# A delta-rule recurrence in chunks: TensorE's, ScalarE's and GpSimd's work put in another order around three crossings

## The chip, the cores and the metric

One core of a Trainium2 chip runs the whole kernel. The metric is the device time of one execution in microseconds (us); the time of a kernel is the median of its runs.

## The reference, cut to what matters

Four layers follow each other on `x` (4 x 1024 x 128, f32). The change touches only the first, a gated delta rule with 16 heads of 64 by 64 state:

```python
q = silu(causal_dwconv(x @ Wq.T)); k = silu(causal_dwconv(x @ Wk.T)) * SCALE
v = silu(causal_dwconv(x @ Wv.T)); a = sigmoid(x @ Wa.T + ba); beta = sigmoid(x @ Wb.T + bb)
def step(S, inp):
    qt, kt, vt, at, bt = inp
    err = einsum('bhij,bhj->bhi', S, kt) - vt
    S = at[..., None] * S - bt[..., None, None] * (err[..., None] * kt[:, :, None, :])
    return S, einsum('bhij,bhj->bhi', S, qt)
o = (layernorm(o, over 64) * ln_w + ln_b) * sigmoid(x @ Wg.T);  return o @ Wo.T
```

The other three (a mixture of experts, banded attention, local attention with its feed-forward) run after it and are left alone.

## The kernel before, in words

Class `DeltaRule` cuts the 1024 steps into 32 chunks of 32 steps (`SEG`), all 4 batches and 16 heads at once, and each chunk into 4 quarters of 8 steps. The five engines run lists written out by hand (`tensor`, `vector`, `scalar`, `gpsimd`, `sync`), in order, and wait for each other only on semaphores. In the names below s is the chunk; `old`, `older` and `nxt` are s-1, s-2 and s+1.

What VectorE does in one chunk is a chain. `dve_P` (L1261) turns the product P of the state with k and q out of banks 4 and 5. Four quarters of single steps follow (`dve_quarter`, L1299 to L1305). After each of the first three comes a **crossing**, which carries a finished quarter over to the steps behind it: VectorE turns W (L1324, into `a_wt`), TensorE multiplies it with the Gram matrix (`pe_cross`, L676, 64 products in banks 6 and 7), and VectorE turns the result (L1347, into `a_cross`). Between L1324 and L1347 VectorE has one to three other operations. After the last quarter `dve_state` turns W once more (L1378), TensorE forms the update U (`pe_U`, L705), ScalarE writes two quarters of the new state (L866), VectorE adds the other two (L1385), and TensorE can form P of the next chunk (`pe_P`, L660: a first half for batches 0 and 1 that waits for ScalarE's part, a second that waits for VectorE's).

Beside this chain TensorE prepares the next chunk and finishes older ones, in the gaps between crossings: projections of a, k, q and v (L572, L559), time rows (L594), Gram products (L584), turns of the normed output (`pe_turn`, L604), the output gate (`pe_gate`, L559 with `a_w_g`), the output product (`pe_out`, L634) and two sums for the norm (L619). These results go to banks 0 and 1 in turn: `take` hands out bank n % 2 and waits until ScalarE has emptied the result two before it. `act_gram` empties one Gram bank with six activations (L799, L801, four on L805); there are two banks per chunk. GpSimd (`pool_...`) makes decays, the rest of P and the output's products. The chain ends for chunk s when the new P is there, so a chunk's length is the distance of two L1261 of channel half 0.

`pe_P` also waits for `("dev", s - 2)`, the second sum of the norm, which VectorE takes at the very end of `dve_state`:

```python
self.dve_out(e, q, s, 1)          # L1371, waits for GpSimd's s_pq (s, 1)
for n in range(2, 4): ...         # L1385, the state
self.dve_values(e, q, s + 1)      # L1228
self.dve_moment(e, q, s - 1, "dev")   # L1244
```

Of the kernel before, what the change touches and what calls it, by code (L numbers as in the profile page):

```python
# [442 lines left out]
class DeltaRule:  # L443
# [194 lines left out]
    def pe_P(self, e, q, s, ch):  # L638
# [7 lines left out]
        else:  # L646
# [4 lines left out]
            if s >= 3:  # L651
                q.wait_ge(self.s_evac, ("out", s - 3))
# [57 lines left out]
    def tensor(self, e, q):  # L710
# [5 lines left out]
        for half in range(2):  # L716
            self.pe_gram(e, q, 0, half)
            self.pe_project_rows(e, q, "v", 0, half)
        for s in range(self.nseg):
            old, older, nxt = s - 1, s - 2, s + 1  # L720
# [35 lines left out]
            self.pe_U(e, q, s)  # L756
        for s in (self.nseg - 2, self.nseg - 1):
# [30 lines left out]
    def act_gram(self, e, q, s, par):  # L788

        heads = slice(8 * par, 8 * par + 8)  # L790
        v = self.held(("gram", s, par)).rearrange("p (r c t z) -> p c r z t", z=2, c=NCK, t=CK)
        dst = self.G1[:, :, :, heads].rearrange("p z t r -> p r z t")
        q.wait_ge(self.s_full, ("gram", s, par))
        if s:
# [3 lines left out]
        rows_of = self.cst["cross_rows"]  # L798
        e.activation(self.Gh[:, :, :, heads].rearrange("p z t r -> p r z t"), v[:, 1], ACT.Identity, scale=rows_of[:, 2:3],  # L799
                     bias=rows_of[:, 3:4]).then_inc(*self.s_gh.at((s, par)))  # L800
# [2263 lines left out]
```

## Time and profile before

| | us |
|---|---|
| median of 3 runs (4098.43 to 4113.96) | 4102.49 |
| the profiled execution | 4110.15 |
| its span in the trace | 4108.4 |
| TensorE, VectorE, GpSimd, ScalarE busy | 3193.8, 2963.0, 2255.2, 2106.6 |
| the recurrence's chunks, start of the first to start of the last | 151 to 2472 |

The span is the profile's own clock from first to last instruction; the execution's time is 1.75 us more. The busy times are over all four layers. The recurrence is read on the timeline of single chunks, which are alike from the fourth on.

### The profile page before, as it was taken

How to read it: one execution, taken by the hardware profiler on the slowest of the kernel's cores; microseconds unless marked ns; L12 is line 12 of the kernel's file. 1: busy time of each engine (PE TensorE's matmuls, PEld its weight loads, DVE VectorE, ACT ScalarE, POOL GpSimd, SP SyncE). 2: the span in 40 equal slices, each digit the busy share in tenths (PEclk: the TensorE clock that was granted, in tenths of full speed). 3: DMA queues.
4: the chain of work that ended last, by engine and by line, in shares of the span. 5: the costliest groups of instructions: out<-in, count | busy, mean ns of one | idle time of the engine just before them, and what ended most of it. 6: DMA issues, size and time to landing. Idle time of an engine off the chain costs nothing. (4 is left out here: it accounts for less than half of the span.)

```text
span 4108.4 us, 125735 instructions
## 1 busy us (share of the span) xinstructions
PE 3193.8 (78%) x53313; PEld 2381.3 (58%) x53313; DVE 2963.0 (72%) x6568; ACT 2106.6 (51%) x4454; POOL 2255.2 (55%) x2831
## 2 busy tenths in 40 slices
PE   4777777677777777777777774468999979998998
PEld 2566565565565655655655654355666647655775
DVE  4587777777787777777877875216888868856885
ACT  2334434444444444443444442335888879937982
POOL 1466666676666666666766765332000068807860
PEclk7888888888888888888888886588999989998999
DMA  2000100100100100001000000510000011101110
GB/s 72 18 29 17 29 19 17 31 17 16 31 17 17 31 17 23 25 17 29 15 15 27 15 15 15 149 41 1 2 2 2 2 34 38 43 6 38 40 37 26
DMA packets 131379, 105.91 MB, mean 26 GB/s; under 512 B 56784, under 2 KB 100044, under 8 KB 130562
## 3 DMA queue, kind: packets, MB, share of 16 engines
q1 hardware_dynamic: 128514, 95.15, 8.7%
q8 instruction: 421, 6.90, 0.7%
q0 software_dynamic: 2304, 2.71, 0.2%
q14 instruction: 140, 1.15, 0.1%
HBM read 62.57 MB, written 16.30 MB: 19 GB/s over the span
## 5 line engine op out<-in xcount | busy, mean ns | idle before, releaser
L1299 DVE TENSOR_TENSOR a_tmp<-a_h,banks 128x128 f32<-128x128 f32 (+6 forms) x896 | 439.2, 490 | 32.9
L1305 DVE TENSOR_REDUCE a_h<-a_tmp 128x64 f32<-128x128 f32 (+6 forms) x896 | 434.4, 485 | 8.8
L1347 DVE STREAM_TRANSPOSE a_cross<-banks 128x1024 f32<-128x1024 f32 x96 | 120.0, 1250 | 309.7 <-PE banks L676 309.7
L660 PE MATMUL banks<-a_st,a_kq 64*32 64x64 f32 x8192 | 179.2, 280 | 176.3 <-DVE a_variance L1244 131.6
L775 ACT ACTIVATE a_kq<-banks 128x512 f32<-128x512 f32 x128 | 82.9, 648 | 392.7 <-PE banks L559 392.7
L978 POOL TENSOR_TENSOR a_h<-a_h,a_a 128x128 f32<-128x128 f32 (+3 forms) x256 | 140.9, 550 | 250.1 <-DVE a_h L1305 250.1
L2196 ACT ACTIVATE c_s<-c_s,c_low 128x384 f32<-128x384 f32 (+1 forms) x512 | 266.3, 579 | 18.9 <-DVE c_low L2140 13.6
L660 PEld LDWEIGHTS banks<-a_st,a_kq 64*32 64x32 f32 x8192 | 166.2, 145 | 188.2 <-DVE a_variance L1244 135.8
L784 ACT ACTIVATE a_va<-banks 128x512 f32<-128x512 f32 x128 | 134.1, 1086 | 274.9 <-PE banks L572 274.8
L559 PEld LDWEIGHTS banks<-a_xseg,a_w_k 128*128 128x128 f32 x2048 | 236.5, 194 | 60.0 <-ACT a_va L784 41.5
L2140 DVE CUSTOM_DVE_ANT_0 c_s<-banks,c_band 128x384 f32<-128x384 f32 (+1 forms) x512 | 245.4, 517 | 24.8 <-PE banks L2065 24.8
L559 PE MATMUL banks<-a_xseg,a_w_k 128*128 128x128 f32 x2048 | 242.6, 278 | 26.2 <-DMA a_xseg<-xn 18.3
L2241 POOL TENSOR_TENSOR c_qm<-c_qT,c_heads 128x512 f32<-128x512 f32 x32 | 33.3, 1040 | 398.4 <-PE banks L2065 398.1
L572 PE MATMUL banks<-a_w_v,a_xseg 128*32 128x512 f32 x2048 | 245.5, 622 | 6.6 <-ACT a_g L805 5.3
L1066 POOL TENSOR_TENSOR a_cross<-a_cross,a_dk 128x128 f32<-128x128 f32 x96 | 54.3, 566 | 338.8 <-DVE a_cross L1347 338.8
L2079 PE MATMUL banks<-k_ident,c_s 128*128 128x128 f32 x1408 | 217.8, 285 | 28.4 <-ACT c_pt L2203 15.6
L559 PE MATMUL banks<-a_xseg,a_w_q 128*128 128x128 f32 x2048 | 234.0, 273 | 0.0
L559 PEld LDWEIGHTS banks<-a_xseg,a_w_q 128*128 128x128 f32 x2048 | 231.3, 191 | 0.2 <-ACT a_kt L824 0.2
L2079 PEld LDWEIGHTS banks<-k_ident,c_s 128*128 128x128 f32 x1408 | 155.4, 143 | 120.0 <-ACT c_s L2196 111.1
L2577 ACT ACTIVATE d_S<-d_S,d_low 128x128 f32<-128x128 f32 x512 | 199.2, 399 | 19.3 <-DVE d_low L2642 18.9
L2426 PE MATMUL banks<-d_wqkv,d_hT 128*128 128x512 f32 x384 | 199.8, 635 | 10.2 <-DVE d_rot L2624 5.9
L1303 DVE TENSOR_TENSOR a_h<-a_h,banks 128x32 f32<-128x32 f32 (+6 forms) x640 | 178.6, 279 | 22.0
(327 smaller groups left out, 9223.8 us busy)
## 6 DMA issues: line engine op xcount, KB each, us to landing
a_ab<-decays SPq DMA_DIRECT2D x256, 128.0 KB, 3.0
d_Vs<-d_V SPq DMA_DIRECT2D x128, 128.0 KB, 2.4
sent<-k_nothing SPq DMA_DIRECT2D x40, 64.5 KB, 2.1
b_xe<-sent SPq DMA_DIRECT2D x8, 322.5 KB, 3.4
a_xseg<-xn SPq DMA_DIRECT2D x32, 70.0 KB, 2.9
a_xrow<-in_L_attn_x SPq DMA_DIRECT2D x128, 16.0 KB, 1.9
x<-a_xrow SPq DMA_DIRECT2D x128, 16.0 KB
back<-k_nothing SPq DMA_DIRECT2D x32, 64.0 KB, 1.6
```

The lines of the kernel that those rows point to most:

```text
L559: t = e.matmul(b[:, m * SW:(m + 1) * SW].rearrange("p (b t) -> p b t", b=NB), self.wT[n][:, j, ct * P:(ct + 1) * P], xs[:, :, off:off + SE ...
L572: t = e.matmul(b[bi * SEG:(bi + 1) * SEG, :], xs[:, bi, off:off + SEG], self.wT[n][:, j, part], start=(j == 0), stop=(j == taps - 1))
L660: t = e.matmul(pb[bi * SEG:(bi + 1) * SEG, at:at + DK], kq[ps, ct * NB + bi, js].rearrange("p t z -> p (t z)"), self.ST[ps, bi * NCT + ct, ...
L978: e.tensor_tensor(self.history(t + 1, lo, t), self.history(t, lo, t), at, ALU.mult).then_inc(*self.s_hist.at((s, t)))
L1299: e.tensor_tensor(prod, both, gram, ALU.mult).then_inc(*step.at((s, t, "product")))
L1303: e.tensor_tensor(self.history(t, lo, t), self.history(t, lo, t), at, ALU.mult).then_inc(*step.at((s, t, "decay")))
L1305: e.tensor_reduce(self.results(t), prod, AX.X, ALU.add).then_inc(*step.at((s, t, "w")))
L2079: t = e.transpose(b[:, j * P:(j + 1) * P], self.S[u % self.NS][:, j * P:(j + 1) * P], self.c.ident[:])
L2140: e.tensor_tensor_reduce(out=self.S[u % self.NS][:, 0:w], in0=self.c.bank(r)[:, 0:w], in1=self.W.band[:, m0:m0 + w], scale=-HD ** -0.5, sc ...
L2196: e.activation(s[:, 0:w], s[:, 0:w], ACT.Exp, scale=-1.0, bias=self.low[u % self.NS][:, 0:1]).then_inc(*self.s_exp.at(u))
L2426: e.matmul(b, self.hT[:, g * P:(g + 1) * P], self.W.wqkv[:, z * INNER:(z + 1) * INNER], start=True, stop=True).then_inc(*self.s_proj.at((g ...
L2577: t = e.activation(s, s, ACT.Exp, scale=-1.0, bias=self.low[g % 2][:, par, r:r + 1], accum_out=self.rows[g % 2][:, par, r:r + 1])
```

## The change

TensorE gets its work around the crossings in another order: time rows ahead of k, half of k behind crossing 0, both gates and no v ahead of crossing 2, and the output product of chunk s-3 (not s-2) between Gram and turns. ScalarE follows that order and empties both Gram banks with six activations of twice the width; the first user of a bank after Gram waits for both. GpSimd makes the output's products one chunk later, around `pool_rest`, and some of its other steps change places. VectorE's list differs at one place, the end of `dve_state`. SyncE's row transfers move a chunk.

```diff
-            q.wait_ge(self.s_evac, self.ring[n - 2])
+            last = self.ring[n - 2]
+            q.wait_ge(self.s_evac, ("gram", last[1], 1) if last[0] == "gram" else last)
...
 def tensor
             self.pe_P(e, q, s, 0)
             self.pe_P(e, q, s, 1)
             if more:
                 for half in range(2):
                     self.pe_project_rows(e, q, "a", nxt, half)
-                for half in range(2):
-                    self.pe_project(e, q, "k", nxt, half)
-            self.pe_cross(e, q, s, 0)
             for n in range(2):
                 self.pe_time_rows(e, q, s, n)
+            if more:
+                self.pe_project(e, q, "k", nxt, 0)
+            self.pe_cross(e, q, s, 0)
             if old >= 0:
                 self.pe_moment(e, q, old, "mean")
             if more:
+                self.pe_project(e, q, "k", nxt, 1)
                 for half in range(2):
                     self.pe_project(e, q, "q", nxt, half)
             self.pe_cross(e, q, s, 1)
             if more:
                 for n in range(2):
                     self.pe_gram(e, q, nxt, n)
+            if oldest >= 0:
+                self.pe_out(e, q, oldest)
             if older >= 0:
                 for n in range(2):
                     self.pe_turn(e, q, older, n)
                 for n in range(2):
                     self.pe_gate(e, q, older, n)
-            if more:
-                self.pe_project_rows(e, q, "v", nxt, 0)
             self.pe_cross(e, q, s, 2)
             if more:
-                self.pe_project_rows(e, q, "v", nxt, 1)
-            if older >= 0:
-                self.pe_out(e, q, older)
+                for half in range(2):
+                    self.pe_project_rows(e, q, "v", nxt, half)
...
 def act_gram (one call for both banks)
+        e.activation(to(self.Gh), v[:, 1], ACT.Identity, scale=rows_of[:, 2:3], bias=rows_of[:, 3:4]).then_inc(*self.s_gh.at(s))
+        e.activation(to(self.G1), v[:, 1], ACT.Copy, scale=-1 / 8).then_inc(*self.s_gwhole.at(s))
+        q.wait_ge(self.s_gwhole, s)
         for bi in range(NB):
             rows = slice(bi * SEG, bi * SEG + CK)
-            t = e.activation(dst[rows], v[rows, 0], ACT.Copy, scale=-1 / 8)
-        t.then_inc(*self.s_evac.at(("gram", s, par)))
+            t = e.activation(to(self.G1)[rows], v[rows, 0], ACT.Copy, scale=-1 / 8)
+            if bi >= 2:
+                t.then_inc(*self.s_evac.at(("gram", s, bi - 2)))
...
 def gpsimd
+            if oldest >= 0:
+                self.pool_gate(e, q, oldest, 0)
             self.pool_rest(e, q, s)
+            if oldest >= 0:
+                self.pool_gate(e, q, oldest, 1)
...
             self.pool_cross(e, q, s, 3)
-            if old >= 0:
-                self.pool_centre(e, q, old, 1)
-            for half in range(2):
-                if older >= 0:
-                    self.pool_gate(e, q, older, half)
             self.pool_older(e, q, s, 1)
...
+                self.pool_gram_rows(e, q, nxt)
+                self.pool_prepare(e, q, nxt, 0)
+            if oldest >= 0:
+                self.pool_add(e, q, oldest)
             self.pool_query(e, q, s, 1)
...
 def dve_state
         self.dve_last(e, q, s, 1)
-        self.dve_out(e, q, s, 1)
+        if s:
+            self.dve_moment(e, q, s - 1, "dev")
+        if s + 1 < self.nseg:
+            self.dve_values(e, q, s + 1)
         for n in range(2, 4):
...
-        if s + 1 < self.nseg:
-            self.dve_values(e, q, s + 1)
-        if s:
-            self.dve_moment(e, q, s - 1, "dev")
+        self.dve_out(e, q, s, 1)
```

TensorE around crossings 0 and 1 of one chunk, before (`a_gx` marks crossings 0 and 2, `a_gh` crossing 1):

```order
L572 MATMUL banks<-a_w_a,a_xseg 32x512 x8
L559 MATMUL banks<-a_xseg,a_w_k 128x128 x32
L676 MATMUL banks<-a_wt,a_gx 32x64 x64
L594 MATMUL banks<-k_ident,a_kq 32x128 x32
L619 MATMUL banks<-a_o_1,k_row_mean 128x128 x8
L559 MATMUL banks<-a_xseg,a_w_q 128x128 x32
L676 MATMUL banks<-a_wt,a_gh 32x64 x64
```

and of the change:

```order
L574 MATMUL banks<-a_w_a,a_xseg 32x512 x8
L596 MATMUL banks<-k_ident,a_kq 32x128 x32
L561 MATMUL banks<-a_xseg,a_w_k 128x128 x16
L678 MATMUL banks<-a_wt,a_gx 32x64 x64
L621 MATMUL banks<-a_o_1,k_row_mean 128x128 x8
L561 MATMUL banks<-a_xseg,a_w_k 128x128 x16
L561 MATMUL banks<-a_xseg,a_w_q 128x128 x32
L678 MATMUL banks<-a_wt,a_gh 32x64 x64
```

Half of k moved behind crossing 0, the time rows ahead of it.

TensorE from Gram to the second sum of the norm, around crossing 2, before:

```order
L584 MATMUL banks<-a_kq 32x64 x64
L604 MATMUL banks<-k_ident,a_o 128x128 x8
L559 MATMUL banks<-a_xseg,a_w_g 128x128 x8
L572 MATMUL banks<-a_w_v,a_xseg 32x512 x16
L676 MATMUL banks<-a_wt,a_gx 32x64 x64
L572 MATMUL banks<-a_w_v,a_xseg 32x512 x16
L634 MATMUL banks<-a_w_o,a_y 128x128 x8
L619 MATMUL banks<-a_o,k_row_mean 128x128 x8
```

and of the change:

```order
L586 MATMUL banks<-a_kq 32x64 x64
L636 MATMUL banks<-a_w_o,a_y 128x128 x8
L606 MATMUL banks<-k_ident,a_o 128x128 x8
L561 MATMUL banks<-a_xseg,a_w_g 128x128 x8
L678 MATMUL banks<-a_wt,a_gx 32x64 x64
L574 MATMUL banks<-a_w_v,a_xseg 32x512 x32
L621 MATMUL banks<-a_o,k_row_mean 128x128 x8
```

One half of v moved from ahead of the crossing to behind it, the output product from behind it to the place behind Gram.

VectorE at the end of a chunk, before:

```order
L1378 STREAM_TRANSPOSE a_wt<-a_h 128x32x32
L1361 TENSOR_TENSOR a_tmp<-a_h,banks 128x256
L1363 TENSOR_REDUCE a_h<-a_tmp 128x32
L1371 TENSOR_TENSOR a_o_1<-a_p_1,a_h 128x32x16
L1385 TENSOR_TENSOR a_st<-a_st,banks 128x512 x2
L1228 STREAM_TRANSPOSE a_bv<-a_va 128x1024
L1244 TENSOR_REDUCE a_variance<-banks 128x32
```

and of the change:

```order
L1391 STREAM_TRANSPOSE a_wt<-a_h 128x32x32
L1374 TENSOR_TENSOR a_tmp<-a_h,banks 128x256
L1376 TENSOR_REDUCE a_h<-a_tmp 128x32
L1257 TENSOR_REDUCE a_variance<-banks 128x32
L1241 STREAM_TRANSPOSE a_bv<-a_va 128x1024
L1401 TENSOR_TENSOR a_st<-a_st,banks 128x512 x2
L1384 TENSOR_TENSOR a_o_1<-a_p_1,a_h 128x32x16
```

The output's subtraction (L1371, now L1384) moved from the first place behind the quarter to the last, the sum and the turn of v ahead of the state's additions.

## Rows read from the trace of the kernel before

**Rows 1.** Timeline of VectorE, first L1261 of the fourth and of the last chunk

```profile
360.51 1.25 DVE L1261 STREAM_TRANSPOSE a_p<-banks 128x1024 f32<-128x1024 f32 x1 [3.36 <-PE banks L660]
...
2472.24 1.25 DVE L1261 STREAM_TRANSPOSE a_p<-banks 128x1024 f32<-128x1024 f32 x1 [3.13 <-PE banks L660]
```

**Rows 2.** Groups of VectorE, 287 to 2472 us: busy us, mean ns | idle before, releaser

```profile
L1347 DVE STREAM_TRANSPOSE a_cross<-banks 128x1024 f32<-128x1024 f32 x87 | 108.7, 1250 | 292.5 <-PE banks L676 292.5
...
L1261 DVE STREAM_TRANSPOSE a_p<-banks 128x1024 f32<-128x1024 f32 x58 | 71.3, 1229 | 95.5 <-PE banks L660 95.5
...
L1371 DVE TENSOR_TENSOR a_o<-a_p,a_h 128x512 f32<-128x512 f32 x58 | 66.5, 1147 | 52.3 <-POOL a_p L1084 52.3
```

**Rows 3.** Timeline of VectorE, one chunk: start, us, instruction [idle before, releaser]

```profile
1039.43 1.25 DVE L1261 STREAM_TRANSPOSE a_p<-banks 128x1024 f32<-128x1024 f32 x1 [3.36 <-PE banks L660]
...
1056.17 1.25 DVE L1347 STREAM_TRANSPOSE a_cross<-banks 128x1024 f32<-128x1024 f32 x1 [2.78 <-PE banks L676]
...
1071.30 1.25 DVE L1347 STREAM_TRANSPOSE a_cross<-banks 128x1024 f32<-128x1024 f32 x1 [0.19 <-PE banks L676]
...
1091.18 1.25 DVE L1347 STREAM_TRANSPOSE a_cross<-banks 128x1024 f32<-128x1024 f32 x1 [6.09 <-PE banks L676]
...
1102.05 1.94 DVE L1378 STREAM_TRANSPOSE a_wt<-a_h 128x1024 f32<-128x1024 f32 x1
...
1106.49 1.44 DVE L1371 TENSOR_TENSOR a_o<-a_p,a_h 128x512 f32<-128x512 f32 x1 [1.80 <-POOL a_p L1084]
1107.86 1.27 DVE L1385 TENSOR_TENSOR a_st<-a_st,banks 128x512 f32<-128x512 f32 x2
...
1113.66 1.25 DVE L1261 STREAM_TRANSPOSE a_p<-banks 128x1024 f32<-128x1024 f32 x1 [3.21 <-PE banks L660]
```

**Rows 4.** Timeline of TensorE, the same chunk

```profile
1046.69 7.41 PE L559 MATMUL banks<-a_xseg,a_w_k 128*128 128x128 f32 x64 [0.34 <-ACT a_va L784]
1054.03 2.06 PE L676 MATMUL banks<-a_wt,a_gx 32*32 32x64 f32 x128
...
1059.80 7.31 PE L559 MATMUL banks<-a_xseg,a_w_q 128*128 128x128 f32 x64
1069.17 2.07 PE L676 MATMUL banks<-a_wt,a_gh 32*32 32x64 f32 x128 [2.06 <-issue]
...
1073.71 0.77 PE L584 MATMUL banks<-a_kq 64*32 64x64 f32 x40 [1.21 <-issue]
...
1079.79 1.12 PE L604 MATMUL banks<-k_ident,a_o 128*128 128x128 f32 x4 [2.62 <-ACT a_g L805]
1081.33 3.78 PE L559 MATMUL banks<-a_xseg,a_w_g 128*128 128x128 f32 x16 [0.42 <-ACT a_oT L882]
1085.04 4.08 PE L572 MATMUL banks<-a_w_v,a_xseg 128*32 128x512 f32 x32
...
1104.04 2.00 PE L705 MATMUL banks<-a_wt,a_kt 32*64 32x64 f32 x128 [1.10 <-DVE a_wt L1378]
1110.51 3.08 PE L660 MATMUL banks<-a_st,a_kq 64*32 64x64 f32 x128 [4.48 <-DVE a_variance L1244]
```

**Rows 5.** Timeline of ScalarE, the same chunk

```profile
1045.57 1.98 ACT L784 ACTIVATE a_va<-banks 128x512 f32<-128x512 f32 x2 [6.76 <-PE banks L572]
...
1072.34 0.80 ACT L799 ACTIVATE a_gh<-banks,k_cross_rows 128x256 f32<-128x256 f32 x1 [1.45 <-PE banks L584]
...
1077.31 2.43 ACT L805 ACTIVATE a_g<-banks 16x256 f32<-16x256 f32 x4
1079.77 2.91 ACT L882 ACTIVATE a_oT<-banks,a_lnb,a_lnw 128x128 f32<-128x128 f32 x8
...
1105.26 1.08 ACT L866 ACTIVATE a_st<-banks 128x512 f32<-128x512 f32 x2 [5.52 <-PE banks L705]
```

**Rows 6.** Timeline of TensorE, P in another chunk

```profile
739.56 1.89 PE L660 MATMUL banks<-a_st,a_kq 64*32 64x64 f32 x128 [1.38 <-DVE a_p L1261]
```

**Rows 7.** Stretches of 3 us: busy us of each engine, granted TensorE clock, DMA

```profile
1078.00:1081.00 3.00, 1.12 (x4) 0.72 (x4) 2.86 (x5) 2.95 (x7) 1.68 (x3) 0.50 0.00 0
...
1087.00:1090.00 3.00, 3.00 (x84) 1.31 (x80) 0.00 (x0) 0.85 (x2) 0.00 (x0) 1.00 0.02 5
```

More of the change, by code:

```diff
@@ L745, in tensor @@
                     self.pe_gate(e, q, older, n)
-            if more:
-                self.pe_project_rows(e, q, "v", nxt, 0)
             self.pe_cross(e, q, s, 2)
             if more:
-                self.pe_project_rows(e, q, "v", nxt, 1)
-            if older >= 0:
-                self.pe_out(e, q, older)
+                for half in range(2):
+                    self.pe_project_rows(e, q, "v", nxt, half)
             if old >= 0:
@@ L756, in tensor @@
             self.pe_U(e, q, s)
+        if self.nseg >= 3:
+            self.pe_out(e, q, self.nseg - 3)
         for s in (self.nseg - 2, self.nseg - 1):
@@ L786, in act_project_rows, with act_gram @@
                      ACT.Sigmoid if n == "a" else ACT.Silu).then_inc(*self.s_evac.at((n, s, half)))
[L788 to L793, printed above, removed]
+    def act_gram(self, e, q, s):
+        assert self.slot[("gram", s, 0)] % 2 == 0
+        v = self.c.bank(0, 2).rearrange("p (r c t z) -> p c r z t", z=2, c=NCK, t=CK)
+        to = lambda x: x[:].rearrange("p z t r -> p r z t")
+        rows_of = self.cst["cross_rows"]
+        for par in range(2):
+            q.wait_ge(self.s_full, ("gram", s, par))
         if s:
@@ L919, in scalar @@
             if more:
+                self.act_project(e, q, "k", nxt, 0)
+            self.act_cross_gram(e, q, s, 2)
+            if more:
+                self.act_project(e, q, "k", nxt, 1)
                 for half in range(2):
@@ L924, in scalar @@
             if more:
-                for n in range(2):
-                    self.act_gram(e, q, nxt, n)
+                self.act_gram(e, q, nxt)
+            if oldest >= 0:
+                self.act_out(e, q, oldest)
             if older >= 0:
@@ L936, in scalar @@
             if more:
-                self.act_cross_gram(e, q, nxt, 0)
-                self.act_project_rows(e, q, "v", nxt, 1)
-            if older >= 0:
-                self.act_out(e, q, older)
+                for half in range(2):
+                    self.act_project_rows(e, q, "v", nxt, half)
             self.act_state(e, q, s)
@@ L1176, in gpsimd @@
             self.pool_cross(e, q, s, 2)
+            self.pool_from_half(e, q, s)
             for t in range(2 * QK + HAND, 3 * QK):
                 self.pool_history(e, q, s, t)
-            self.pool_from_half(e, q, s)
             self.pool_next(e, q, s, 1)
-            if old >= 0:
-                self.pool_centre(e, q, old, 0)
+            for half in range(2):
+                if old >= 0:
+                    self.pool_centre(e, q, old, half)
             self.pool_cross(e, q, s, 3)
-            if old >= 0:
-                self.pool_centre(e, q, old, 1)
-            for half in range(2):
-                if older >= 0:
-                    self.pool_gate(e, q, older, half)
             self.pool_older(e, q, s, 1)
@@ L1192, in gpsimd @@
                 self.pool_cumulate(e, q, nxt, 2, QK)
+                self.pool_gram_rows(e, q, nxt)
+                self.pool_prepare(e, q, nxt, 0)
+            if oldest >= 0:
+                self.pool_add(e, q, oldest)
             self.pool_query(e, q, s, 1)
             if more:
-                self.pool_prepare(e, q, nxt, 0)
-                self.pool_gram_rows(e, q, nxt)
                 self.pool_values(e, q, nxt)
-            if older >= 0:
-                self.pool_add(e, q, older)
+        if self.nseg >= 3:
+            for half in range(2):
+                self.pool_gate(e, q, self.nseg - 3, half)
+            self.pool_add(e, q, self.nseg - 3)
         if self.nseg >= 2:
@@ L1455, in sync @@
         self.spread_decays(e, q, 0)
-        for s in range(self.nseg + 2):
+        for s in range(self.nseg + 3):
             if s + 1 < self.nseg:
@@ L1460, in sync @@
                 self.load(e, s + 1)
-            if s >= 2:
-                self.get_rows(e, q, s - 2)
-            self.fill.piece(e, s)
+            if s >= 3:
+                self.get_rows(e, q, s - 3)
+            if s < self.nseg + 2:
+                self.fill.piece(e, s)
             if s + 1 < self.nseg:
```

37 lines of the change are left out of this document (16 added, 21 removed).

## The prediction

> **What bounds the kernel now.** I read the timeline of VectorE first, from the fourth chunk's P to the last one's [rows 1]: 2472.24 - 360.51 = 2111.7 us for 28 chunks, 75.4 us each. That is half of the span, and it is the only part that the change touches. Then the groups of VectorE with the idle time before them [rows 2]: over 29 chunks it waits 292.5 us for the crossings, 95.5 for P and 52.3 for GpSimd's query part, together 440, or 15.2 us a chunk. The rest, some 60 us, is VectorE's own work, so VectorE is the bound with gaps in it, and no order of the other engines gives back more than those 15.2.
>
> One chunk shows where the gaps lie [rows 3]. I call T the start of L1261, X0, X1 and X2 the three starts of L1347, and w the end of L1378 (1102.05 + 1.94 = 1103.99). The legs are T to X0 16.7 (waits 2.78), X0 to X1 15.1 (0.19), X1 to X2 19.9 (6.09), X2 to w 12.8, w to the next T 9.7 (1.80 and 3.21); sum 74.2. The timeline of TensorE says why [rows 4]. Crossing 0 starts at 1054.03, right behind the k projection, though its operand was ready before: TensorE was late. Crossing 1 starts after 2.06 us of idle time, as soon as its operand is there. Behind it come Gram, turns that wait for ScalarE, gates and half of v, and crossing 2 can start only when that half (1085.04 + 4.08) is done. At the chunk's end, P of the next one waits 4.48 us until VectorE has done the norm's sum.
>
> **The change, leg by leg.** Instruction counts stay, but for ScalarE's Gram copies, six fewer a chunk.
>
> *T to X0.* Half of k (7.41 / 2 = 3.7) leaves the place ahead of crossing 0, and the time rows come there, 1.9 (they and the mean's sum fill the 3.8 us between crossing 0 and q, two like pieces) [rows 4]. Crossing 0, at T + 14.6, could start at T + 12.8, X0 at T + 14.95. P ahead of it takes 3.1 us in most chunks and 1.89 in one where the clock was full [rows 4, 6]; with that, TensorE is early, and VectorE's own end of work sets X0: 1056.17 - 2.78 is T + 13.95. The a projection's wait for its transfer goes as well, since GpSimd's add, behind which SyncE issues that transfer, now stands ahead of its query part and not behind its values. I take 14.3, between 13.95 and 14.95.
>
> *X0 to X1.* TensorE has between crossings 0 and 1 now the mean 1.9, half of k 3.7 and q 7.3, 12.9 us; VectorE's turned W comes 12.9 us after X0 (crossing 1 starts at 1069.17, X0 at 1056.17). The 2 us of slack are used up. 15.1 stays; from 15.1 to 16.5.
>
> *X1 to X2.* The new list up to crossing 2: Gram ends 3.2 us after X1 (1073.71 + 0.77), a stall of 1.21 in it [rows 4]. ScalarE took from 1072.34 to 1079.74 for twelve copies of 256 columns [rows 5], 0.6 each. The six of 512 are not in the trace. The nearest row is L784, 512 columns with a strided output: 1.98 for two [rows 5]. I take 0.98 each and 6.0 for six; the ends are 3.9 (0.65 each, as if the stride cost nothing) and 7.3 (twice 0.6 each). The output product of s-3, 2.05, hides beside them. So the banks are free at X1 + 9.3, and both turns wait for that. A turn is 1.12 at the low clock, four of the eight copies on L882 1.5, a gate half of 3.78: 9.4 + 1.1 + 1.5 + 1.9 + 1.9 = X1 + 15.8 [rows 4, 5], crossing 2 is 2.06, X2 = X1 + 18.0; without the stall 16.9. VectorE is free at X1 + 13.8 (1091.18 - 6.09), so it still waits some 4 us. I take 17.6 instead of 19.9. What pays is not the shorter emptying alone: 4.1 us of v are no longer ahead of the crossing.
>
> The Trainium skill's page "ScalarE: Activation LUTs" (section "What ACT_TABLE_LOAD costs") gives an activation with immediate operands as 186 ns plus 0.833 ns a column. For 256 columns that is 0.40 us where the trace shows 0.6, so the row speaks against it for these strided copies. By the page the six would take 3.7 us and X2 would come 2.3 us earlier, about 65 us over the kernel.
>
> *X2 to w* stays at 12.8. Behind crossing 2 TensorE has v 7.3, the norm's sum 2 and the carry 1.9, 11.2 in all, and 1.6 of slack before U. GpSimd's chain to the query's end keeps its length: two halves of y and one centring leave it, the Gram rows, the preparation and the add come into it, about 3.8 against 3.7 us.
>
> *w to T.* VectorE's last reduction ends at w + 0.7 (1106.49 - 1.80). Now the norm's sum (0.24) and v's turn (1.2) follow, during U's 2.00 us, then the state's additions, 1.27, to w + 3.4 [rows 3, 4]. ScalarE's half of the state is there at w + 2.35 [rows 5], so the first half of P runs beside the additions and the second ends at w + 4.4 at full clock, w + 5.6 at low. The subtraction that waited for GpSimd is last: 1.44, to w + 4.8; GpSimd's query part, which it met at w + 2.5 before, is long done by then. I take 4.9 instead of 9.7; from 4.8 to 5.7.
>
> New chunk: 14.3 + 15.15 + 17.6 + 12.8 + 4.9 = 64.75. The average chunk before was 1.2 above the one I read, from transfer waits and stalls of TensorE; I keep half, 65.4. That is 10.0 less for 28 chunks, 281. The first three chunks gain mostly at their ends, the last one at crossing 0, 20 together; behind the loop the output of one more chunk is left, +3. Sum: 4110.2 - 298 = 3812 for the profiled execution. It lay 7.7 above the median, so 3804.
>
> **The rivals.**
> - *Full clock between the crossings.* If TensorE keeps 2.4 GHz through turns and gates, these halve: turn 0.56, a gate 0.95, and P at the full clock. X1 to X2 becomes 15.6, T to X0 14.0, the chunk 63.0: 12.4 x 28 + 20 = 367 less, 3736. Against it: the granted clock was 0.50 there after idle times of 2 to 3 us [rows 7], and the change leaves one of some 4 us in the same place. Chance 0.12.
> - *TensorE is the bound.* With no slack ahead of crossings 0 and 1, every stall like the 1.21 in Gram [rows 4] is on the path, and turns and gates are. Three more a chunk, 1.1 each, make 68.7: 6.7 x 28 + 15 = 203 less, 3900. For it: the average chunk before is 1.2 us above the one read [rows 1, 3], so such stalls are there. Chance 0.25.
> - *The low clock stays (slower).* The idle time between the output product and the turns lets the clock fall to 1.2 GHz, as rows 7 show at 1078; before, it was back at 1.00 at 1087. If it came back only behind U, v, sum and carry would take 22 us, U would be 9.4 us late and P 0.8: the gain is gone. If it also stayed low through part of k and q of the next chunk, each microsecond of that work costs one more, and 1 to 2 us a chunk give about +40, 4145. It decides from the point at which the low stretch, some 10 us before, lasts over 20. Against it: P now follows U almost at once, where the clock used to fall too. Chance 0.05.
> - *No change.* The waits return elsewhere, GpSimd the likeliest place, since its list is as long as before in a shorter chunk. Chance 0.03.
>
> The Trainium skill's page "TensorE: Matmul & The Clock Gate" (section "The HAM clock gate") calls the throttled state the default, released by activity; that is the ground of the slower rival, and the trace agrees that the clock falls behind idle stretches.
>
> **How the numbers follow.** The forecast has 0.55, with 3770 to 3850 as its own range. Predicted time 3804. The range 3735 to 3900 takes in the full clock on one side and the stalls on the other. Below 0.5% (20 us) a measurement of this kernel tells nothing; faster is the first three cases, 0.92, same 0.03, slower 0.05.
>
> **What would show it.** In the profile after: distance of P to P about 65 us; idle before L1347 about 0.5, 0.5 and 4 us; no wait of P for the norm's sum; VectorE's output subtraction without idle time; the strided Gram copies near 1 us each; turns behind both Gram banks. Wrong, if crossing 1 waits for q by more than 1 us on average, if the copies take 0.65, if the clock row between Gram and gates reads 1.00, or if w to T stays above 7.

## The result, and the profile after

| | before | changed |
|---|---|---|
| median, us | 4102.53 (4 runs) | 3905.78 (4 runs, 3899.87 to 3914.52) |
| profiled execution, us | 4110.15 | 3908.86 |
| TensorE, VectorE, GpSimd, ScalarE busy, us | 3193.8, 2963.0, 2255.2, 2106.6 | 3193.8, 2970.4, 2258.5, 2078.5 |

The ratio is 0.9518, its 95% interval 0.9491 to 0.9545: 4.8% faster. The forecast was 3804 and the range ended at 3900, 6 us short. Busy times hardly moved, so all of it is waiting. The timeline of VectorE in the changed kernel, with the first L1274 (the old L1261) of the fourth and the last chunk, and between them the main rows of one chunk; L1360 is the old L1347, L1391 the old L1378, L1401 the old L1385, L1384 the old L1371:

```profile
355.41 1.25 DVE L1274 STREAM_TRANSPOSE a_p<-banks 128x1024 f32<-128x1024 f32 x1 [1.99 <-PE banks L662]
...
966.00 1.25 DVE L1274 STREAM_TRANSPOSE a_p<-banks 128x1024 f32<-128x1024 f32 x1 [1.61 <-PE banks L662]
...
981.01 1.25 DVE L1360 STREAM_TRANSPOSE a_cross<-banks 128x1024 f32<-128x1024 f32 x1 [1.07 <-PE banks L678]
996.20 1.25 DVE L1360 STREAM_TRANSPOSE a_cross<-banks 128x1024 f32<-128x1024 f32 x1 [0.19 <-PE banks L678]
...
1014.54 1.25 DVE L1360 STREAM_TRANSPOSE a_cross<-banks 128x1024 f32<-128x1024 f32 x1 [4.67 <-PE banks L678]
1025.42 1.99 DVE L1391 STREAM_TRANSPOSE a_wt<-a_h 128x1024 f32<-128x1024 f32 x1
...
1029.50 1.29 DVE L1401 TENSOR_TENSOR a_st<-a_st,banks 128x512 f32<-128x512 f32 x2
1030.70 1.77 DVE L1384 TENSOR_TENSOR a_o<-a_p,a_h 128x512 f32<-128x512 f32 x1
...
1034.12 1.25 DVE L1274 STREAM_TRANSPOSE a_p<-banks 128x1024 f32<-128x1024 f32 x1 [1.65 <-PE banks L662]
...
2262.28 1.25 DVE L1274 STREAM_TRANSPOSE a_p<-banks 128x1024 f32<-128x1024 f32 x1 [2.15 <-PE banks L662]
```

(2262.28 - 355.41) / 28 = 68.1 us a chunk, against 75.4 [rows 1]. The same reading of all 28 chunks, fourth to last but one, gives the legs that the prediction used (T the start of P's turn, X0 to X2 the starts of the three crossings' turns, w the end of the last turn of W, taken in every run as its start + 1.94 us as in [rows 3]; in the changed kernels that turn lasts up to 0.1 us longer, so that the true X2 to w is that much longer and w to T that much shorter):

| mean of a leg, us | before | forecast | after |
|---|---|---|---|
| T to X0 | 17.07 | 14.3 | 14.76 |
| X0 to X1 | 15.41 | 15.15 | 15.23 |
| X1 to X2 | 20.38 | 17.6 | 18.46 |
| X2 to w | 12.81 | 12.8 | 12.83 |
| w to T | 9.75 | 4.9 | 6.83 |
| chunk | 75.42 | 64.75, with stalls 65.4 | 68.10 |

The groups of VectorE, 287 to 2262 us, answer to [rows 2]: waits for crossings 292.5 to 168.0, for P 95.5 to 43.5, for GpSimd's query part 52.3 to nothing.

```profile
L1360 DVE STREAM_TRANSPOSE a_cross<-banks 128x1024 f32<-128x1024 f32 x87 | 108.7, 1250 | 168.0 <-PE banks L678 167.3
L1384 DVE TENSOR_TENSOR a_o<-a_p,a_h 128x512 f32<-128x512 f32 x59 | 72.4, 1226 | 0.0
L1274 DVE STREAM_TRANSPOSE a_p<-banks 128x1024 f32<-128x1024 f32 x58 | 71.2, 1228 | 43.5 <-PE banks L662 43.5
```

The sum: 28 chunks give 28 x 7.32 = 205 us, the first three 10. Ahead of the loop 5.1 are lost (the first P is turned at 156.55 instead of 151.45: v now waits for both Gram banks), behind the last chunk's w 5.2, and 3.5 in the other layers. 205 + 10 - 14 = 201, the difference of the two profiled executions. Ahead of the loop TensorE stands idle for 6.4 us ahead of v, until ScalarE has emptied Gram.

TensorE in the chunk above, to be laid beside [rows 4]:

```profile
975.11 3.84 PE L561 MATMUL banks<-a_xseg,a_w_k 128*128 128x128 f32 x32
978.87 2.07 PE L678 MATMUL banks<-a_wt,a_gx 32*32 32x64 f32 x128
...
994.08 2.06 PE L678 MATMUL banks<-a_wt,a_gh 32*32 32x64 f32 x128 [0.44 <-issue]
...
998.90 0.64 PE L586 MATMUL banks<-a_kq 64*32 64x64 f32 x29 [1.34 <-issue]
...
1006.01 1.97 PE L606 MATMUL banks<-k_ident,a_o 128*128 128x128 f32 x8 [4.48 <-ACT a_g L811]
1008.72 3.75 PE L561 MATMUL banks<-a_xseg,a_w_g 128*128 128x128 f32 x16 [0.74 <-ACT a_oT L889]
1012.40 2.07 PE L678 MATMUL banks<-a_wt,a_gx 32*32 32x64 f32 x128
...
1027.47 2.00 PE L707 MATMUL banks<-a_wt,a_kt 32*64 32x64 f32 x128 [2.29 <-DVE a_wt L1391]
1029.92 2.59 PE L662 MATMUL banks<-a_st,a_kq 64*32 64x64 f32 x100 [0.46 <-ACT a_st L873]
1033.01 1.07 PE L662 MATMUL banks<-a_st,a_kq 64*32 64x64 f32 x28 [0.50 <-issue]
```

Crossing 0 still starts right behind k, but behind half of it. Crossing 1 has 0.4 us of idle time ahead of it where it had 2. Crossing 2 starts right behind the gates, which are slow. P follows U after 0.46, is slow too, and stops once inside. The stretches say how fast the clock was (columns as in [rows 7]):

```profile
1002.00:1005.00 3.00, 0.00 (x0) 0.00 (x0) 2.83 (x6) 2.95 (x4) 1.32 (x3) 1.00 0.00 0
1005.00:1008.00 3.00, 1.97 (x8) 1.57 (x8) 2.93 (x3) 2.07 (x5) 2.84 (x4) 0.58 0.01 3
1008.00:1011.00 3.00, 2.28 (x10) 2.28 (x11) 1.87 (x3) 2.98 (x7) 3.00 (x3) 0.50 0.00 0
1026.00:1029.00 3.00, 1.53 (x112) 1.53 (x114) 2.97 (x5) 0.30 (x1) 2.84 (x6) 1.00 0.50 169
1029.00:1032.00 3.00, 2.54 (x126) 2.43 (x121) 2.97 (x4) 2.48 (x7) 2.76 (x3) 0.56 0.60 186
```

It fell to 1.2 GHz (0.50) in the 4.5 us idle ahead of the turns. It fell again near the end of U, which has 2.3 us of idle time ahead of it, in the middle of the chain's end. ScalarE in the same chunk:

```profile
999.64 1.24 ACT L806 ACTIVATE a_gh<-banks,k_cross_rows 128x512 f32<-128x512 f32 x1 [3.84 <-PE banks L586]
...
1001.80 4.16 ACT L811 ACTIVATE a_g<-banks 16x512 f32<-16x512 f32 x4
```

Six wide copies, 999.64 to 1005.96: 6.3 us, about 1.05 each, near the 6.0 forecast.

### The profile page after: what moved, and what is told of

It is laid out like the page before. It is cut to its first block and busy times, and to the rows that moved or that the text cites. A ratio compares the mean times of both kernels' runs of the same rounds, so it can differ in the third digit from the quotient of the medians.

```text
span 3907.1 us, 125601 instructions
## 1 busy us (share of the span) xinstructions
PE 3193.8 (82%) x53313; PEld 2407.0 (62%) x53313; DVE 2970.4 (76%) x6568; ACT 2078.5 (53%) x4262; POOL 2258.5 (58%) x2831
## 5 line engine op out<-in xcount | busy, mean ns | idle before, releaser
L789 ACT ACTIVATE a_va<-banks 128x512 f32<-128x512 f32 x128 | 135.3, 1108 | 243.8 <-PE banks L574 243.8
L1360 DVE STREAM_TRANSPOSE a_cross<-banks 128x1024 f32<-128x1024 f32 x96 | 120.0, 1250 | 185.1 <-PE banks L678 184.3
L561 PE MATMUL banks<-a_xseg,a_w_k 128*128 128x128 f32 x2048 | 244.8, 276 | 17.6 <-DMA a_xseg<-xn 17.6
L662 PE MATMUL banks<-a_st,a_kq 64*32 64x64 f32 x8192 | 195.1, 284 | 75.8 <-DVE a_p L1274 44.1
L574 PE MATMUL banks<-a_w_v,a_xseg 128*32 128x512 f32 x2048 | 229.4, 600 | 6.4 <-ACT a_g L811 6.4
L662 PEld LDWEIGHTS banks<-a_st,a_kq 64*32 64x32 f32 x8192 | 175.9, 148 | 93.6 <-DVE a_p L1274 50.8
L1337 DVE STREAM_TRANSPOSE a_wt<-a_h 128x1024 f32<-128x1024 f32 x96 | 191.3, 1993 | 3.3
```

The lines of the kernel that those rows point to most:

```text
L561: t = e.matmul(b[:, m * SW:(m + 1) * SW].rearrange("p (b t) -> p b t", b=NB), self.wT[n][:, j, ct * P:(ct + 1) * P], xs[:, :, off:off + SE ...
L574: t = e.matmul(b[bi * SEG:(bi + 1) * SEG, :], xs[:, bi, off:off + SEG], self.wT[n][:, j, part], start=(j == 0), stop=(j == taps - 1))
L662: t = e.matmul(pb[bi * SEG:(bi + 1) * SEG, at:at + DK], kq[ps, ct * NB + bi, js].rearrange("p t z -> p (t z)"), self.ST[ps, bi * NCT + ct, ...
L1337: e.transpose(self.Wt[:].rearrange("p x i -> p i x"), self.W).then_inc(*self.s_wm.at((s, n)))
```

## The experiments

All ratios are to the kernel before, run beside the variant on the same chip; the change itself is 0.9518 (0.9491 to 0.9545). Legs are means over the same 28 chunks.

### Undoing one part at a time

**state_old**: the old order at the end of `dve_state`.

```diff
         self.dve_last(e, q, s, 1)
-        if s:
-            self.dve_moment(e, q, s - 1, "dev")
-        if s + 1 < self.nseg:
-            self.dve_values(e, q, s + 1)
+        self.dve_out(e, q, s, 1)
...
-        self.dve_out(e, q, s, 1)
+        if s + 1 < self.nseg:
+            self.dve_values(e, q, s + 1)
+        if s:
+            self.dve_moment(e, q, s - 1, "dev")
```

> The change, but with the old order at the end of dve_state (output subtraction first, norm's sum last). If the new order is what shortens w to the next P (9.75 us before, 6.83 after), that leg comes back to 9 to 9.7 us and the time to about 3905 + 29 x 2.5 = 3980. Rival: the leg is short because GpSimd's query part is done earlier and VectorE no longer waits for it; then the old order costs little, since the subtraction does not wait: leg about 8, time about 3935.

0.9621 (0.9599 to 0.9643), median 3951.57. w to T went to 8.89 us, T to X0 fell a little, to 14.31. The leg lies just below the first forecast, the time between the two. So the order is worth 2.06 us of that leg, but 1.5 of the chunk (69.62): part of it is eaten up at crossing 0. The leg's other 0.86 us of gain do not hang on the order; with the old order the subtraction still waits for GpSimd, 36.8 us in all instead of 52.3.

**v_ahead**: the first half of v ahead of crossing 2, on TensorE and ScalarE.

```diff
+            if more:
+                self.pe_project_rows(e, q, "v", nxt, 0)
             self.pe_cross(e, q, s, 2)
             if more:
-                for half in range(2):
-                    self.pe_project_rows(e, q, "v", nxt, half)
+                self.pe_project_rows(e, q, "v", nxt, 1)
... (ScalarE's list likewise)
```

> The change with the first half of v back ahead of crossing 2 on TensorE and ScalarE. If v ahead of the crossing is what cost the old X1 to X2, the crossing comes 3.7 to 4.1 us later: X1 to X2 about 22.3, time about 3905 + 29 x 3.8 = 4015, nearly the whole gain of that leg and more. Rival: TensorE would have that time again behind the crossing; it has slack there, so nothing comes back. Within 1% of 3905 only if the gates and not v set crossing 2.

0.9778 (0.9752 to 0.9804), median 4016.39; X1 to X2 22.37, 3.9 us more, and T to X0 14.32, 0.4 less; the chunk is 3.56 longer. As expected: what stands ahead of the crossing in the list is paid nearly in full.

**k_ahead**: both halves of k ahead of crossing 0.

```diff
                 self.pe_project(e, q, "k", nxt, 0)
+                self.pe_project(e, q, "k", nxt, 1)
             self.pe_cross(e, q, s, 0)
...
-                self.pe_project(e, q, "k", nxt, 1)
... (ScalarE's list likewise)
```

> The change with both halves of k ahead of crossing 0. T to X0 grows by 3.7 us less the slack that is there, from 14.8 to about 18.0; X0 to X1 stays 15.2 (TensorE then has 3.7 us of slack ahead of crossing 1). Time about 3905 + 29 x 3.2 = 3998. Rival: the slack gained ahead of crossing 1 gives something back; time below 3960.

0.9778 (0.9752 to 0.9805), median 4014.21; T to X0 18.29, X0 to X1 16.04, X1 to X2 17.66. The first figure is as expected; the other two were not forecast, and nearly cancel. The traces say where they come from. TensorE now stands idle for 3.94 us ahead of crossing 1:

```profile
1040.70 2.81 PE L678 MATMUL banks<-a_wt,a_gh 32*32 32x64 f32 x128 [3.94 <-issue]
```

The granted clock is 0.65 on average in that crossing, where it is 1.00 in the change, and its products take 2.99 us instead of 2.07. Behind it Gram's issue waits, here in k_ahead and then in the change, are nearly gone:

```profile
L586 PE MATMUL banks<-a_kq 64*32 64x64 f32 x3712 | 76.7, 263 | 1.4 <-issue 1.4
```

```profile
L586 PE MATMUL banks<-a_kq 64*32 64x64 f32 x3712 | 63.7, 222 | 31.5 <-issue 31.5
```

The chunk is 3.46 longer. The three parts undone by themselves (order, v, k) cost 8.5 us of a chunk together, more than the 7.32 of the whole change, so they are not independent of each other.

**gram_narrow**: both banks emptied together, by twelve copies of 256 columns.

```diff
+        h = (slice(0, 8), slice(8, 16))
...
+            e.activation(to(self.G1)[rows, h[0]], v[rows, 0, h[0]], ACT.Copy, scale=-1 / 8)
+            t = e.activation(to(self.G1)[rows, h[1]], v[rows, 0, h[1]], ACT.Copy, scale=-1 / 8)
```

> The change with both Gram banks emptied together, but by twelve copies of 256 columns instead of six of 512. If the wide copies save 1.1 us a chunk (7.4 against 6.3 us in the traces) and the turns wait for their end, X1 to X2 grows from 18.5 to 19.6 and the time by 29 x 1.1 = 32 us, to about 3937. Rival: the gain of the joined emptying lies elsewhere; within 10 us of the change.

0.9511 (0.9487 to 0.9535): no difference. ScalarE's timeline shows first and last of the twelve:

```profile
1069.22 0.78 ACT L807 ACTIVATE a_gh<-banks,k_cross_rows 128x256 f32<-128x256 f32 x1 [3.69 <-PE banks L586]
...
1075.04 0.62 ACT L815 ACTIVATE a_g<-banks 16x256 f32<-16x256 f32 x1
```

1069.22 to 1075.66 is 6.44 us, against 6.32 for six wide ones. The narrow ones start 0.40 and 0.65 us after each other in turn, though each lasts 0.6. My expectation took 7.4 for twelve from the old trace; that was the time of two separate emptyings, in which the copies ran one behind the other. In this order of twelve the width brings nothing.

**pool_old**: GpSimd's old order behind crossing 2 and for Gram rows and preparation.

```diff
-            self.pool_from_half(e, q, s)
             for t in range(2 * QK + HAND, 3 * QK):
                 self.pool_history(e, q, s, t)
+            self.pool_from_half(e, q, s)
...
-                self.pool_gram_rows(e, q, nxt)
-                self.pool_prepare(e, q, nxt, 0)
             if oldest >= 0:
                 self.pool_add(e, q, oldest)
             self.pool_query(e, q, s, 1)
             if more:
+                self.pool_prepare(e, q, nxt, 0)
+                self.pool_gram_rows(e, q, nxt)
```

> The change with GpSimd's list back in the old order at two places: the rest of the half chunk behind the four histories and the second centring behind crossing 3; Gram rows and preparation behind the query part. If GpSimd was never what the chain waits for, nothing changes (within 10 us of 3905). Rival: X2 waits for the rest of the half (from_half), or ScalarE's bank of Gram rows for the next chunk comes too late and holds the first quarter; 20 us or more slower.

0.9514 (0.9498 to 0.953), median 3906.98: GpSimd's order at these places is free. Its y one chunk later, and the output product with it, was not undone by itself.

**add_late**: GpSimd's add behind the values.

```diff
-            if oldest >= 0:
-                self.pool_add(e, q, oldest)
             self.pool_query(e, q, s, 1)
             if more:
                 self.pool_values(e, q, nxt)
+            if oldest >= 0:
+                self.pool_add(e, q, oldest)
```

> The change with GpSimd's add back behind the values, at the end of its chunk. The add releases SyncE, which then issues the transfer of a_xseg. If its earlier place is needed for the change to pay, the a projection waits for the transfer again, about 3 us a chunk: T to X0 from 14.8 to about 17.5, time about 3905 + 29 x 2.7 = 3983. Rival: with the output product in the middle of the chunk SyncE is early enough in any case; within 10 us of 3905.

0.9525 (0.9509 to 0.9541), median 3912.55. The wait for a_xseg came back in 14 of 28 chunks, 14.1 us in all, and T to X0 rose by 0.4. The rival was right: in this kernel the place of the add matters little.

### One part alone: a gain that goes elsewhere

**state_alone**: the kernel before with only the new end of `dve_state` (the diff of that function as it stands in the change).

> The kernel before with only the new order at the end of dve_state. If the order itself gives the shorter end of the chunk, w to P falls from 9.75 to 6.5 to 7 us with everything else as before, time 4111 - 29 x 3 = about 4024. Rival: without GpSimd's earlier query part and the idle crossings the end is bound elsewhere; w to P above 8.5, time above 4075.

0.9986 (0.9974 to 0.9998), median 4099.95. This is the most telling run. w to T fell from 9.75 to 6.14 us, even below the 6.5 to 7 expected, and T to X0 rose from 17.07 to 20.80. TensorE's timeline in a chunk of state_alone shows the new wait:

```profile
1032.45 1.89 PE L660 MATMUL banks<-a_st,a_kq 64*32 64x64 f32 x128 [1.37 <-DVE a_p L1261]
1038.67 3.64 PE L572 MATMUL banks<-a_w_a,a_xseg 128*32 128x512 f32 x16 [4.33 <-DMA a_xseg<-xn]
```

The transfer is issued by SyncE behind the row stores of chunk s-2, and these wait for GpSimd's add, last in its list, which did not move. P came 3.6 us earlier, the a projection did not, and in the idle time the clock fell too (3.64 us instead of 1.93; granted clock 0.50 in the stretch 1039 to 1042).

**state_load**: state_alone, and the load ahead of the row stores.

```diff
+        self.load(e, 1)
         for s in range(self.nseg + 2):
-            if s + 1 < self.nseg:
-                if s >= 3:
-                    q.wait_ge(self.s_full, ("g", s - 3, 1))
-                self.load(e, s + 1)
...
+            if s + 2 < self.nseg:
+                if s >= 2:
+                    q.wait_ge(self.s_full, ("g", s - 2, 1))
+                self.load(e, s + 2)
             if s >= 2:
                 self.put_rows(e, q, s - 2)
```

> The kernel before with the new order at the end of dve_state, and with SyncE's load of a_xseg for the chunk after next issued ahead of the row stores (so that it waits no longer for GpSimd's add). In state_alone the 3.6 us saved at the chunk's end came back as a later X0, with the a projection waiting 3.2 us for that transfer. If the transfer is the cause, T to X0 falls from 20.8 to about 17, w to P stays near 6.1, time 4100 - 29 x 3.8 = about 3990. Rival: the k projection itself is late because it starts a fixed time after P; then P, a and k all simply start earlier and the time is near 4000 as well only if P runs at full clock; at the low clock T to X0 stays above 19 and the time above 4045.

0.9754 (0.9738 to 0.9771), median 4005.56; T to X0 16.66, w to T 6.16, chunk 71.29. The transfer was the cause of the lost gain: the same edit that was worth nothing is worth 2.3% once the load is moved ahead in the queue. The earlier load alone, in the kernel before, was not run; there the a projection waits for its transfer 27.4 us in all, 0.7% of the time, so it could give little more than that by itself. The a projection's groups in state_alone and state_load, 287 to 2262 us:

```profile
L572 PE MATMUL banks<-a_w_a,a_xseg 128*32 128x512 f32 x432 | 88.2, 956 | 80.8 <-DMA a_xseg<-xn 80.8
```

```profile
L572 PE MATMUL banks<-a_w_a,a_xseg 128*32 128x512 f32 x448 | 63.3, 680 | 16.9 <-DMA a_xseg<-xn 15.6 <-issue 1.2
```

### The chunk's end: clock or stalls

**small_ab**: the decays' transfers made small.

```diff
...
+                if s:
+                    src, dst = src[:, 0:32], dst[:, 0:32]
...
```

> The change, with the transfers that spread the decays over the partitions cut from 128 KB to 8 KB each from the second chunk on (their count and waits stay; the decays of the state are then wrong). Theory B, TensorE's stalls marked 'issue' inside P come from instruction delivery that shares the DMA engines with these transfers: the stalls in P go, w to P falls from 6.8 to about 6.0, time about 3880. Theory A, P is slow because the granted clock fell to 1.2 GHz in the 2.3 us of idle time before U: nothing changes by more than 0.3%.

0.9483 (0.9461 to 0.9504), median 3894.55; w to T 6.47. P's issue waits went from 18.6 to 14.9 us. That is neither of the two forecasts: the traffic has a small share at most, and the intervals overlap with the change's.

**warm_u** and **warm_t**: products of the identity that nobody uses, in TensorE's idle time ahead of U, or ahead of the turns.

```diff
+    def pe_warm(self, e, q, s, n, bank):
+        ...
+        for _ in range(n):
+            e.matmul(b[:, 384:512], self.c.ident[:], self.c.ident[:], start=True, stop=True)
...
             self.pe_carry(e, q, s)
+            self.pe_warm(e, q, s, 8, 5)
             self.pe_U(e, q, s)
```

> The change, with 8 extra products of the identity (about 1.8 us at full clock, into bank 5, used by nobody) between the carry and U, in TensorE's idle time. Theory A (the clock falls in that idle time, and P then runs at 1.2 GHz): the granted clock stays at 1.00 through U and P, P takes about 1.9 us of work instead of 3.6, w to P falls from 6.83 to 5.1 to 5.5 us and T to X0 from 14.76 to about 14.1, time about 3905 - 29 x 2.2 = 3842. Theory B (instruction delivery): w to P stays above 6.3, time within 0.5% of 3905.

0.9476 (0.9454 to 0.9497), median 3894.55. w to T only 6.43: P ran at the faster clock in most chunks, and waited longer inside. The interval touches that of the change.

> The change, with 14 extra products of the identity (about 3.2 us at full clock, into bank 4, used by nobody) before the turns, where TensorE stands idle 4.5 us while ScalarE empties Gram. If the clock is what makes turns and gates slow there: both turns 1.0 instead of 2.0 us, both gates 1.9 instead of 3.75, X1 to X2 from 18.46 to about 16.5, time about 3905 - 29 x 2 = 3847. If ScalarE's norm copies and not the clock set the gates: X1 to X2 stays above 17.8, time above 3885.

0.9432 (0.941 to 0.9453), median 3872.25. X1 to X2 17.49, between the two forecasts: both turns took 1.1 instead of 2.0 us, but the gates, with 1.2 us of idle time ahead of them, were at the low clock again in 15 of 28 chunks.

**thin_U** and **thin_warm**: U without 7 of 8 head pairs of batches 0 and 1, so that their state is not updated; the second with warm_u's products as well.

```diff
+                        if pair == 0 and ct < NCT - 1:
+                            continue
```

> The change with 56 of the 64 products of U that belong to batches 0 and 1 in pairs left out (7 of 8 head pairs; their state is then not updated). The waits marked issue come in bursts of small products: Gram's behind crossing 1, P's behind U. If they are TensorE's instruction supply running behind a burst, P's wait for issue (18.6 us in 28 chunks, longest 2.5) nearly vanishes, Gram's stays at 1.1 a chunk, and w to P falls from 6.8 to about 5.5. Rival, the decays' transfers or anything tied to the time of day in the chunk: P's issue wait stays.

One run, 3863.76: w to T 5.56, as expected.

> thin_U and warm_u together: no burst of U ahead of P, and TensorE busy ahead of U. My step that failed said that the chunk's end would take 4.9 us, with P at full clock and without stall; it takes 6.8. thin_U alone gave 5.6, warm_u alone 6.4. If clock and supply stall together are the whole cause, both away give P's 1.9 us of work without issue wait, and the leg is set by VectorE's subtraction, 5.1 us or less. If it stays at 5.5 or above, something else is in it.

One run, 3854.54: w to T 5.26, between the two forecasts (5.1 and 5.5). P's groups, 290 to 2200 us, in the change, in warm_u, in thin_U and in thin_warm:

```profile
L662 PE MATMUL banks<-a_st,a_kq 64*32 64x64 f32 x7296 | 174.0, 284 | 68.0 <-DVE a_p L1274 39.5 <-issue 18.6 <-ACT a_st L873 9.7
```

```profile
L662 PE MATMUL banks<-a_st,a_kq 64*32 64x64 f32 x7216 | 150.4, 257 | 87.6 <-DVE a_p L1285 38.6 <-issue 36.0 <-ACT a_st L884 12.9
```

```profile
L662 PE MATMUL banks<-a_st,a_kq 64*32 64x64 f32 x7284 | 167.5, 276 | 49.8 <-DVE a_p L1276 39.3 <-ACT a_st L875 4.5 <-issue 4.0
```

```profile
L662 PE MATMUL banks<-a_st,a_kq 64*32 64x64 f32 x7191 | 135.4, 235 | 76.7 <-DVE a_p L1287 45.4 <-DVE a_st L1414 13.1 <-issue 11.8
```

Work and issue waits of one P (128 records) come to 3.38 us in the change, 3.31 in warm_u, 3.01 in thin_U and 2.62 in thin_warm. A faster clock alone turns work into waiting; a shorter burst ahead of P alone leaves P slow; both together bring 0.76 us. That is still above the 1.9 us without a wait that were expected: issue waits are left (11.8 us), and a wait for VectorE's additions (13.1) is new. But P is hardly late any more. The idle time ahead of its turns is 4.4 us in all, against 42.2 in the change, and in 18 of 28 chunks there is none:

```profile
1015.08 1.25 DVE L1287 STREAM_TRANSPOSE a_p<-banks 128x1024 f32<-128x1024 f32 x1 [0.29 <-PE banks L662]
```

```profile
L1287 DVE STREAM_TRANSPOSE a_p<-banks 128x1024 f32<-128x1024 f32 x57 | 69.8, 1225 | 4.4 <-PE banks L662 4.2
```

There VectorE's own subtraction ends the leg in most chunks. A thinner U is also 0.6 us shorter, so not all of the 1.3 us between 6.83 and 5.56 is stall.

### A version that beats both

**warm_all** fills three idle stretches, **wide_warm** the same with fewer, wider products, **wide_pro** has v ahead of Gram before the loop besides.

```diff
+            self.pe_warm(e, q, s, 14, 4)   # ahead of pe_turn
+            self.pe_warm(e, q, s, 4, 4)    # ahead of pe_gate
+            self.pe_warm(e, q, s, 7, 5)    # ahead of pe_U
```

> The change with extra products of the identity in three idle stretches: 14 ahead of the turns, 4 between turns and gates, 7 ahead of U. If the clock is all that makes these places slow: gates at 1.9 instead of 3.75 us, X1 to X2 16.3, w to P 6.3, T to X0 14.5, chunk 65.1, time about 3905 - 29 x 3.0 = 3818. Rival: the extra instructions lengthen the supply stalls (as in warm_u: P's issue waits 36 instead of 19 us) and ScalarE's norm copies set the gates; chunk above 66.5, time above 3860.

0.9336 (0.9319 to 0.9353), median 3838.24; X1 to X2 16.72, w to T 6.39, chunk 65.76; the time lies between the two forecasts. At turns and gates the clock stays, and a gate's products go from 427 to 286 ns each:

```profile
1050.00:1053.00 3.00, 1.58 (x14) 1.39 (x14) 2.86 (x5) 2.50 (x5) 2.18 (x4) 1.00 0.00 0
1053.00:1056.00 3.00, 2.49 (x20) 2.11 (x19) 3.00 (x3) 2.98 (x8) 2.92 (x4) 1.00 0.00 0
```

```profile
L561 PE MATMUL banks<-a_xseg,a_w_g 128*128 128x128 f32 x464 | 67.2, 286 | 14.7 <-ACT a_oT L902 14.7
```

The Trainium skill's page "TensorE: Matmul & The Clock Gate" (section "The HAM clock gate") says that activity releases a throttled default state. By that rule useless products may pay; by this trace they do, 1.9% of the time at these places (0.9336 against 0.9518).

```diff
-            e.matmul(b[:, 384:512], self.c.ident[:], self.c.ident[:], start=True, stop=True)
+            e.matmul(b, self.c.ident[:], self.woT[:, 0:4, :].rearrange("p c d -> p (c d)"), start=True, stop=True)
```

> As warm_all, but the extra products have 512 moving columns (0.94 us each instead of 0.23), so 2 ahead of U, 3 ahead of the turns, 1 ahead of the gates: 6 instead of 25 products. If warm_all paid for its extra instructions with supply stalls, P's issue waits fall from 33 to about 19 us in 28 chunks, the chunk from 65.8 to about 65.2, time about 3825. Rival: the stalls come from U and P alone; same as warm_all, 3838 within 8 us.

0.9342 (0.9321 to 0.9363), median 3837.46. P's issue waits were 36.8 us, not 19, with 6 filler products a chunk, and 33.0 with the 25 of warm_all: the number of the filler's instructions is not what stalls P. The rival was right.

> wide_warm, and ahead of the loop v in front of Gram on all engines (in the change the first P is 5.1 us later than before, because v waits for both Gram banks). The first P comes 3 to 4 us earlier, nothing else changes: 4 us less than wide_warm. Rival: the Gram rows are then what comes last, no gain.

0.9343 (0.9328 to 0.9359), median 3837.10. The first P came 1.4 us earlier than in wide_warm, not 3 to 4, and the time is the same. The rival was right here too: VectorE now turns the Gram rows last, at 154.25, just ahead of P.

## Why the prediction was wrong

The direction and the places held, and so did the mechanism up to crossing 2 and the last turn of W; at the chunk's end it did not. Forecast 298 us less, measured 201. The 97 between them are 28 x 2.7 = 76 in the chunks and 21 around them.

- **The bound and the gaps** held: VectorE, with its waits at crossings 0 and 2 and at P. The k and v steps held: undone, each cost 2.7% of the change's time. None of the four signs of being wrong showed, though w to T, at 6.83, came near its 7.
- **w to T is the step that failed**: 4.9 was written, 6.83 measured. That is 1.93 of the 3.35 us between 64.75 and 68.10 (0.65 of them had been allowed for as stalls). 1.51 of the 1.93 is VectorE's idle time ahead of P's turn, which was forecast as none. The other 0.42 is its own work, mostly the output subtraction: 1.70 on average where 1.44 was written. In state_alone it takes 0.72; what lengthens it is open. "The second ends at w + 4.4 at full clock, w + 5.6 at low" left P's end, w + 6.7 on average, out of its range, for two reasons.
- **First, the clock.** "1.89 in one where the clock was full" is the P of the other channel half [rows 6]; the P that ends this leg ran at the low clock in all 28 chunks before, and in 26 of 28 after. I took the idle time away behind U and thought that this would keep the clock. But in the chunk of [rows 4] U ends at 1106.04, and the granted clock from 1106 to 1108 is 0.61 on average: it fell some 0.4 us behind U already, early in the 4.48 us of idle time. I had written down 1.6 us of slack ahead of U and gave it no price. It grew from 1.1 to 2.3 us. TensorE has more work behind crossing 2 than before, not less, but it no longer waits for GpSimd in the middle of it, and the idle time is now in one piece ahead of U. That wait in the chunk read before:

```profile
1097.38 2.05 PE L634 MATMUL banks<-a_w_o,a_y 128*128 128x128 f32 x16 [2.69 <-POOL a_y L1092]
```

With this stretch filled (warm_u) P is at the low clock in 7 of 28 chunks. The growth itself is not the whole of it: state_load has only 0.87 us ahead of U, and P at the low clock in 17 of 28 chunks and a leg of 6.16.

- **Second, the issue waits.** P followed U at once, in one burst of small products, which brought issue waits into P, 0.66 us a chunk. It had not had them before:

```profile
L660 PE MATMUL banks<-a_st,a_kq 64*32 64x64 f32 x7448 | 165.4, 283 | 168.5 <-DVE a_variance L1244 128.9 <-DVE a_p L1261 39.7
```

thin_warm takes most of both away. P then ends at w + 4.9 on average, and the leg is 5.26, nearly all of it VectorE's own time.

- **X1 to X2** was written 17.6, between 16.9 without a stall in Gram and 18.0 with it. It has that stall in 27 of 28 chunks, and measured 18.46. Here the term was right and its share wrong. Most of the 0.46 us beyond it are the six wide copies, 6.3 for 6.0. Their width brought nothing: gram_narrow shows that twelve narrow ones, emptied together, take as long.
- **T to X0**, 14.3 against 14.76: the half of k weighed as forecast; P stayed at the low clock in most chunks, which I had only in the upper end.
- **X0 to X1** and **X2 to w** held within 0.1 us.
- **The transfer of a_xseg** I passed with a sentence ("goes as well"). In the change that was right (of 27.4 us of waits for it none is left), but the reason given, the add's earlier place, explains about half of it: add_late puts the add back, and 14.1 us return. What gives the other half was not run by itself. state_alone shows how much hung on the transfer: without the moved work around it, the 3.6 us at the chunk's end are worth nothing.
- **Around the chunks** I counted 17 us of gain and got 3.7 of loss, 21 apart. Of the 20 for the first three chunks and the last, the first three gave 10 and the last one nothing, v behind both Gram banks cost 5.1 ahead of the loop, which the prediction had not looked at, and the tail cost 5.2 instead of 3; 3.5 lie in the other layers and are open.
- **The rivals.** The one that gave 3900 named a bound on TensorE through stalls and slow gates, and this is nearest to what happened, though with one new stall a chunk and not three. The slower one saw the clock fall, but in one place only, and at each of them it came back.

That the instruction supply is what "issue" means there is my reading. Shown is that these waits follow the length of the run of small products (thin_U) and grow when the products are faster (18.6 us in the change, 36.0 in warm_u), and that they hang hardly on the transfers' size (small_ab) and not on the filler's instruction count (wide_warm).

## What to carry to other kernels

Read the end of a chain in both directions: whatever is made earlier must find every other input earlier too, down to the queue that issues its transfer, or the gain only changes its place. Work or a wait that leaves an engine ahead of a critical step leaves idle time there, and on TensorE that idle time has a price in the steps behind it; fill it, or price them at the low clock. In an in-order list, what stands just ahead of a step that others wait for costs its full length, so move that first.

## What the runs showed of the hardware that was not expected

- Copies of 256 strided columns on ScalarE start 0.40 and 0.65 us apart in turn while each lasts 0.6 (gram_narrow); in total twelve took 6.44 us and six of 512 columns 6.32.
- Issue waits appeared inside P as soon as it followed U directly, up to 2.5 us. There were none before, and none in state_old, where P waits for VectorE. Gram, right behind crossing 1, has 0.8 to 1.2 us of them a chunk in every kernel here but k_ahead, where 3.9 us of idle time and a lower clock stand ahead of it and they are 0.05.
- The clock need not fall in the long idle time itself: in the change it fell near U's end, with TensorE at work (0.56 from 1029 to 1032), and before some 0.4 us behind U, with 1.1 us of idle time ahead of U.
- 25 useless products a chunk (warm_all) made the kernel 1.9% faster than the change.
